# One row tile fewer in the experts, another order of VectorE's work and a hand-written last unit in the second layer

## The reference

```
# layer 0, on xn = layernorm(x)
q, k, v = split(xn @ W);  q = elu(q) + 1;  k = elu(k) + 1
s = (q @ (k^T v)) / (q . sum(k) + 1e-6)                       # linear attention, per batch row
e = argmax(xn @ gate_w^T)                                     # one of 8 experts per token
f = (square(relu(g)) * u) @ wd[e],  g = xn @ wg[e],  u = xn @ wu[e]
x = x + s * silu(f)

# layer 1, on xn = layernorm(x)
q, k, v = split(xn @ W_qkv)
p = exp(causal scores of blocks of 128 tokens - row maximum);  p = p / (sum(p) + 1e-6)
s = (p @ v) @ W_out^T + b_out
f = layernorm(xn + outs) * ln_g + ln_b     # outs: attention over the tokens that 16 heads chose
x = x + s * silu(f)
```

## Time and profile before

| | us |
|---|---|
| median of 3 runs | 522.12 (520.51 to 523.44) |
| the profiled execution | 517.94 |
| its span (first to last instruction) | 516.2 |
| TensorE busy | 499.0 (97%) |
| VectorE busy | 456.9 (89%) |
| ScalarE busy | 393.1 (76%) |
| GpSimd busy | 307.5 (60%) |
| granted TensorE clock, mean | 0.998 of full speed |

### The profile page before, as it was taken

The page is one execution under the profiler, slowest core; times in us unless marked ns, Lnnn a source line. Parts: engine busy times, 40 slices in busy tenths (PEclk is TensorE's granted clock), DMA queues, the critical chain, the costliest instruction groups (busy, mean ns, idle before and its releaser), DMA issues.

```text
span 516.2 us, 12184 instructions
## 1 busy us (share of the span) xinstructions
PE 499.0 (97%) x3576; PEld 461.1 (89%) x3576; DVE 456.9 (89%) x1420; ACT 393.1 (76%) x891; POOL 307.5 (60%) x367
## 2 busy tenths in 40 slices
PE   6899999999999999899999999999999999999995
PEld 5899999999999999799999988878888888888884
DVE  6899999999999987669988948989999999999985
ACT  4878878787878774567777856878888887888883
POOL 5568866777676877332222038887777787785200
PEclk9999999999999999999999999999999999999999
DMA  8942322222222115457778664266666555655311
GB/s 228 243 118 88 123 84 81 84 83 83 83 84 83 43 62 193 135 164 237 224 229 262 197 196 124 89 131 139 132 139 137 123 135 131 142 134 111 83 42 62
DMA packets 59415, 67.83 MB, mean 131 GB/s; under 512 B 11864, under 2 KB 53728, under 8 KB 59360
## 3 DMA queue, kind: packets, MB, share of 16 engines
q1 hardware_dynamic: 44416, 38.82, 24.7%
q0 software_dynamic: 14944, 28.32, 22.7%
HBM read 39.85 MB, written 27.26 MB: 130 GB/s over the span
## 4 chain that ended last, share of the span: by engine, by line
PE 78%; DVE 6%; SPq 6%; issue 3%; DMA 3%; ACT 1%; POOL 1%; POOLq 0%; DVEq 0%
PE v_ps L1464 9%; PE q_ps L1442 9%; PE s_ps L1484 5%; PE k_ps L168 3%; PE gu_ps L1123 3%; PE k_ps L169 3%; PE m_ps L168 3%; PE k_ps L170 3%; PE m_ps L170 3%; PE m_ps L169 3%; PE tq_ps L168 3%; PE tq_ps L169 3%; PE tq_ps L170 3%; PE tq_ps L400 3%; PE pa_ps L1495 3%
## 5 line engine op out<-in xcount | busy, mean ns | idle before, releaser
L1816 POOL DMA_INDIRECT four<-expert_rows,gather_u x64 | 69.5, 1086 | 38.1 <-DMA expert_rows<-y 19.5
L949 POOL DMA_INDIRECT sorted_rows<-xn,row_u x64 | 68.0, 1063 | 17.2 <-issue 13.9
L938 POOL TENSOR_TENSOR xn<-xn 128x512 fp32r<-128x512 f32 x32 | 43.2, 1350 | 30.7 <-ACT xn L563 30.4
L1464 PE MATMUL v_ps<-wvo,xt 128*128 128x256 f32 x256 | 60.6, 379 | 0.0
L1442 PE MATMUL q_ps<-xt,wqk 128*128 128x256 f32 x256 | 60.6, 379 | 0.0
L1579 ACT ACTIVATE xn2nd<-res,shift,rstd 128x256 f32<-128x256 f32 (+1 forms) x64 | 34.9, 593 | 26.7 <-DVE shift L1686 26.6
L1442 PEld LDWEIGHTS q_ps<-xt,wqk 128*128 128x128 f32 x256 | 48.5, 190 | 6.9 <-issue 0.4
L209 POOL DMA_DIRECT2D four<-sorted_rows x36 | 19.7, 548 | 56.6 <-issue 53.4
L1464 PEld LDWEIGHTS v_ps<-wvo,xt 128*128 128x128 f32 x256 | 46.3, 190 | 5.0
L1822 POOL DMA_DIRECT2D res<-in_L_attn_x x26 | 35.1, 1391 | 17.6 <-DVE res L1642 16.0
L1831 POOL TENSOR_TENSOR rstd<-var_eps,neg_half 128x4 f32<-128x4 f32 x32 | 36.6, 1143 | 11.9 <-DVE var_eps L1678 11.8
(11 more groups left out here) (260 smaller groups left out, 1748.1 us busy)
## 6 DMA issues: line engine op xcount, KB each, us to landing
expert_rows<-y SPq DMA_DIRECT2D x36, 256.0 KB, 3.1
four<-in_L_attn_x SPq DMA_DIRECT2D x32, 256.0 KB, 2.9
out_rows<-att SPq DMA_DIRECT2D x32, 256.0 KB, 2.1
res<-in_L_attn_x POOLq DMA_DIRECT2D x26, 256.0 KB, 4.9
four<-sorted_rows SPq DMA_DIRECT2D x36, 128.0 KB, 2.6
four<-sorted_rows POOLq DMA_DIRECT2D x36, 128.0 KB, 2.8
wdn<-in_L_ffn_wd SPq DMA_DIRECT2D x2, 512.0 KB, 7.4
sorted_rows<-res SPq DMA_DIRECT2D x8, 128.0 KB, 5.8
```

Of the source, the lines that this page charges most:

```text
L938: nc.gpsimd.tensor_tensor(xn2[:, s, 1], xn[:, i], xn2[:, s, 0].bitcast(F32), ALU.subtract).then_inc(g["xn_split"], 1)
L949: nc.gpsimd.indirect_dma_start(out=z.sorted_dram.ap(), out_offset=bass.IndirectOffsetOnAxis(ap=row_u[:, i // CU, k:k + 1], axis=0), in_=xn ...
L1464: m = nc.tensor.matmul(v_ps[:, t, :], xt[:, i % 2, k, t * P:(t + 1) * P], wvo[:, k, :], start=(t == 0 and k == 0), stop=(k == KD - 1), ski ...
L1816: nc.gpsimd.indirect_dma_start(out=moe[:, n % SLOTS, t, :], out_offset=None, in_=z.expert_dram.ap(), in_offset=bass.IndirectOffsetOnAxis(a ...
```

## The change

- `experts`: a helper `width(n)` gives 1 for the pair 35 and 2 for every other. All helpers and the store handle `width(n)` tiles, so the 72nd row tile is neither computed nor stored. The gather reads from the first 71 tiles of `expert_rows`.
- VectorE's step in `second_layer`: `base_divisor(n-1)` moves up between `norm_stats` and `stats_complete`; `invert_divisor(n-1)` moves from behind `maximum` to behind `find_moments`; `prepare_norm` moves behind `norm_shift`.
- First units: `norm_shift(2)` moves from step 0 to between `scale_rows(4)` and `sum_x(4)`. On GpSimd `add_x(6)` moves ahead of `gather(9)`.
- Last unit (31): the engines' steps run to unit 30, and the rest is written out tile by tile: `v` in two halves with `scores(31)` between them, each probability tile transposed, copied and multiplied by itself, with own PSUM banks for the two tiles, and two stores instead of one.

```diff
+    def width(n):
+        return 1 if isinstance(n, int) and n == PAIRS - 1 else 2
...
-                for u in range(2):
+                for u in range(width(n)):
...
                 if not normed:
                     norm_stats(*ahead)
+                base_divisor(*back)
+                if not normed:
                     stats_complete(*ahead)
                 gate(*back)
                 if not normed:
                     find_moments(*ahead)
-                base_divisor(*back)
+                invert_divisor(*back)
+                if not (isinstance(n, int) and n < 1):
+                    norm_shift(n + 2, at(i, 2))
                 if not normed:
                     prepare_norm(*ahead)
-                if not (isinstance(n, int) and n < 0):
-                    norm_shift(n + 2, at(i, 2))
                 scale_gate(*next_one)
                 maximum(n, i)
-                invert_divisor(*back)
                 gate_rows(*back)
...
-            first_rows(4, 4)
+            scale_rows(4, 4)
+            norm_shift(2, 2)
+            sum_x(4, 4)
...
+            add_x(6)
             gather(9)
-            add_x(6)
```

The last unit. TensorE, then ScalarE, VectorE and SyncE:

```diff
-            run(pe, 0, step, UNITS)
+            run(pe, 0, step, LAST - 1)
+            q(n, i)
+            last_value(0)
+            scores(n, i)
+            turn_probs(n - 1, at(i, -1))
+            last_value(1)
+            attend(n - 1, at(i, -1))
+            pe.wait_ge(g["pt_copied"], n)
+            for t in range(UT):
+                pe.wait_ge(g["p_ready"], UT * n + t + 1)
+                nc.tensor.transpose(last_pt[t], pr[:, i % 2, t, :], z.ident[:]).then_inc(g["pt_ready"], 1)
+            for t in range(UT):
+                pe.wait_ge(g["pt_copied"], n + t + 1)
+                pe.wait_ge(g["v_copied"], n + t + 1)
+                pe.wait_ge(g["a_begun"], n + t + 1)
+                nc.tensor.matmul(last_a[t], prt[:, i % 2, t, :], vo[:, i % 2, t, :], start=False, stop=True,
+                                 skip_group_check=True).then_inc(g["att_ready"], 1)
...
-            run(act, -1, step, UNITS)
+            run(act, -1, step, LAST - 1)
+            tanh(n, i)
+            begin_last(0)
+            copy_q(n, i)
+            exp(n - 1, at(i, -1))
+            last_copy(0, "v_ready", last_v, vo, "v_copied")
+            copy_probs(n - 1, at(i, -1))
+            begin_last(1)
+            exp(n, i)
+            last_copy(1, "v_ready", last_v, vo, "v_copied")
+            for t in range(UT):
+                last_copy(t, "pt_ready", last_pt, prt, "pt_copied")
...
-            run(dve, 3, step, UNITS + 1)
+            run(dve, 3, step, LAST - 1)
+            result(n - 2, at(i, -2))
+            gate(*back)
+            gate(n, i)
+            base_divisor(*back)
+            maximum(n, i)
+            invert_divisor(*back)
+            base_divisor(n, i)
+            gate_rows(*back)
+            invert_divisor(n, i)
+            result(*back)
+            for t in range(UT):
+                dve.wait_ge(g["att_ready"], n + t + 1)
+                nc.vector.scalar_tensor_tensor(att[:, i % SLOTS, t, :], last_a[t], inv[:, i % SLOTS, t:t + 1], zg[:, i % SLOTS, t, :], ALU.mult, ALU.mult).then_inc(g["gated"], 1)
+            for t in range(UT):
+                dve.wait_ge(g["gated"], n + t + 1)
+                nc.vector.tensor_tensor(att[:, i % SLOTS, t, :], att[:, i % SLOTS, t, :], z.res[:, UT * n + t, :], ALU.add).then_inc(g["out_ready"], 1)
...
+            for t in range(UT):
+                sp.wait_ge(g["out_ready"], LAST + 1 + t)
+                sp.dma_start(out_units[LAST][:, t], att[:, LAST % SLOTS, t]).then_inc(out_stored[LAST % SLOTS], 16)
```

More of the change, by code:

```diff
@@ L1017, in experts @@
     assert PAIRS == ROUNDS * QUAD and OWNERS + OCTET * len(OWNER_LOADS) == SLOTS
+    assert z.B * z.L % P == 0
+    def width(n):
+        return 1 if isinstance(n, int) and n == PAIRS - 1 else 2
     with ExitStack() as ctx:
@@ L1153, in experts_of @@
             def experts_of(n):
-                return [pe.snap(owners[(2 * n + u) % OWNERS], min_val=0, max_val=E - 1) for u in range(2)]
+                return [pe.snap(owners[(2 * n + u) % OWNERS], min_val=0, max_val=E - 1) for u in range(width(n))]
             def step(m):
@@ L1429, in sync @@
                 load(n, n)
-            run(sp, 0, step, UNITS + 1)
+            run(sp, 0, step, UNITS)
+            for t in range(UT):
+                sp.wait_ge(g["out_ready"], LAST + 1 + t)
+                sp.dma_start(out_units[LAST][:, t], att[:, LAST % SLOTS, t]).then_inc(out_stored[LAST % SLOTS], 16)
             for i in range(SLOTS):
-                sp.wait_ge(out_stored[i], 16 * UNITS // SLOTS)
+                sp.wait_ge(out_stored[i], 16 * (UNITS // SLOTS + (UT - 1 if i == LAST % SLOTS else 0)))
         def tensor(pe):
@@ L1544, in tensor, with last_value @@
             pe.wait_ge(g["folded_copied"], 2)
-            run(pe, 0, step, UNITS)
+            run(pe, 0, step, LAST - 1)
+            n, i = LAST, LAST % TURN
+            def last_value(t):
+                if t == 0:
+                    pe.wait_ge(g["v_copied"], n)
+                for k in range(KD):
+                    m = nc.tensor.matmul(last_v[t], xt[:, i % 2, k, t * P:(t + 1) * P], wvo[:, k, :], start=(k == 0), stop=(k == KD - 1))
+                m.then_inc(g["v_ready"], 1)
+            q(n, i)
[14 more added lines that the diff above has]
+                                 skip_group_check=True).then_inc(g["att_ready"], 1)
         def scalar(act):
@@ L1634, in scalar, with last_copy, begin_last @@
             act.wait_ge(z.set_up, 4)
-            run(act, -1, step, UNITS)
+            run(act, -1, step, LAST - 1)
+            n, i = LAST, LAST % TURN
+            def last_copy(t, ready, src, dst, done):
+                act.wait_ge(g[ready], n + t + 1)
+                nc.scalar.activation(dst[:, i % 2, t], src[t], ACT.Copy).then_inc(g[done], 1)
+            def begin_last(t):
+                if t == 0:
+                    act.wait_ge(g["gated"], n - 1)
+                else:
+                    act.wait_ge(g["q_copied"], n + 1)
+                nc.scalar.activation(last_a[t], z.eps_bias[:], ACT.Copy).then_inc(g["a_begun"], 1)
+            tanh(n, i)
[9 more added lines that the diff above has]
+                last_copy(t, "pt_ready", last_pt, prt, "pt_copied")
         def vector(dve):
```

47 lines of the change are left out of this document (32 added, 15 removed).

## The result

The changed kernel took 514.34 us, the median of 3 runs (513.58 to 514.72), against 522.12 us (520.51 to 523.44) before. The ratios here are as recorded and are not the quotients of the two medians; in this case the quotient is 0.985, inside the interval, and by the ratio the gain is 6.6 us and not 7.8.

What follows compares the result with a forecast made beforehand. TensorE, busy 97%, was taken as the bound, with VectorE holding the steady steps by a hair. Gains of 1.0 + 2.1 + 0.9 + 1.7 = 5.7 us took 522.12 to 516.4 us, range 513.8 to 520.2.

Steps and rivals of the forecast that it cites:

- Part 1: End of the experts: dropping the 72nd row tile brings the second layer's values 1.0 us earlier, bounds 0 and 1.3.
- Part 2 (a): First units: moving `norm_shift(2)` ahead of `sum_x(4)` and `centre_gate(1)` starts TensorE's turn earlier and saves 0.73 us.
- Part 2 (b): First units: issuing `add_x(6)` ahead of `gather(9)` removes VectorE's wait and TensorE's 1.53 us too-long step.
- the 0.15 for what is late next: First units: with the stall gone, `norm_shift(5)` and the normalising make TensorE's turn late, costing 0.1 to 0.2 us.
- nothing stalls: First units: `gather(9)` comes 1.4 us later, but its rows are used some 6 us after issue, so no wait follows.
- Part 3: Steady steps: VectorE's reordered list falls to about 5.68 us, TensorE becomes the bound, 0.9 us gained, bounds 0 and 1.2.
- rival A: Steady steps: VectorE's order gives nothing, steps stay at 5.93; total gain 4.2 us, 517.9 us; chance 0.15.
- Part 4: Last unit, 31: earlier scores, tile-by-tile work and a half-size last store save 1.7 us, bounds 0.8 and 2.1.
- B: Experts: the dropped tile is off the path, so its 1.0 us is not gained; 517.4 us; chance 0.12.
- C: First units and last unit: the change doesn't win there; total gain 1.9 us, 520.2 us; chance 0.12.
- D: Steady steps: `base_divisor` in its new place closes a loop through the exponentials; slower, 526.5 us; chance 0.04.
- such an offset is the same for both kernels: Total: the median's 4.2 us above the profiled execution was taken as unchanged, turning 512.2 us into 516.4 us.

Runs made afterwards that it cites:

- e3: The changed kernel with all 72 row tiles in the experts again; median 514.88 us, ratio to before 0.9928.
- e5: The changed kernel with GpSimd's `norm_scale(6)` moved ahead of `gather(10)`; median 514.68 us, ratio to before 0.9874.
- e6: The changed kernel with GpSimd's order `gather(10)`, `norm_scale(6)`, `add_x(8)`, so `add_x(8)` comes later; median 514.50 us, ratio to before 0.9874.
- e10: The same kernel as e6, run again on another chip beside the changed kernel; median 515.24 us, ratio to before 0.9899.
- e2: The changed kernel with VectorE's order in a step as before, all else as changed; median 513.37 us, ratio to before 0.9898.
- e7: The changed kernel with the last unit as before, loops running over unit 31 and one store; median 516.02 us, ratio to before 0.9896.
- e4: The changed kernel with `add_x(6)` behind `gather(9)` again; median 516.68 us, ratio to before 0.9967.
- e1: The changed kernel run again with no edit; median 514.55 us, ratio to the kernel before 0.9935.
- e11: The kernel before with one edit, `add_x(6)` ahead of `gather(9)`; median 518.68 us, ratio to before 0.9970.

## Why the prediction was right, point by point

**Part 1**, 1.0 forecast, 0.75 measured (e3 alone: 0.7 to 0.8). The half `gate_up` and the half `down` came as worked out, 0.45 and 0.24 to 0.25. What was mis-sized is the head start of 0.45 that `hidden(35)` was to have on VectorE. Ahead of it stand `silu(32)` and `silu(33)`, at 0.69 each and unchanged: `hidden(35)` starts on VectorE 1.23 us behind `gate_up(35)` (296.25), when the `silu` at 295.64 lets it, against 1.40 before (296.17), so 0.17 earlier where I had 0.45. The halved instructions gave 0.34 where I had 0.35: `hidden_rest(35)` starts 2.98 us behind `gate_up(35)` and not 3.36, of which 0.21 is theirs, and it is itself shorter, which gives 0.13. So `down(35)` comes 0.17 + 0.34 = 0.51 earlier and not 0.8.

**Part 2 (a)**, 0.73 forecast, 0.72 measured. `norm_shift(2)` at 322.67 ended the wait of the turn, with no other one behind it.

**Part 2 (b)**, 1.38 forecast after the 0.15 for what is late next, 1.34 measured at its own place. But the step "nothing stalls" behind `gather(9)` failed. I had asked when the gathered rows were wanted and not what else stands in GpSimd's list. Two gathers took 2.23 and 2.06 us instead of 1.0, `norm_scale(6)` slid to 346.86, and 1.1 us went at unit 6. The forecast's row showed the transfer; the row I lacked is GpSimd's own timeline of the next units, which up to the end of `norm_scale(6)` has no idle stretch over 0.31 us even before (334.30 to 345.73). Neither of the two other orders of GpSimd's list tried here, e5 and e6 with e10, avoids the debt for certain: one execution of e6 did better by 0.6, the next did not.

**Part 3**, 0.9 forecast, 1.07 measured, 5.873 us with VectorE's list at 5.65 and 0.22 of room. My working was loose: the three savings that it names, 0.12, 0.12 and 0.04, add up to 0.28 and not to the 0.23 that it goes on with, and the list fell by 0.26, from 5.91 to 5.65. For the size of the gain this hardly counts, since TensorE holds the step from 5.87 down. e2 decides between this part and rival A: the same instructions with the waits moved apart take 0.27 less a step. For the rival I had taken from the Trainium skill, "VectorE: DVE Perf Modes", section "The DRAIN you can't avoid", that waits cost nothing. That was half of what the section says: it also says that a next instruction that isn't held starts earlier, and with that half the trace agrees (0.05 us from the reciprocal to its follower, 0.19 where the follower waits). Rival A is refuted for the steps. In the total, though, e2 is only 0.5 to 0.7 behind, for part of it is what the stall at unit 6 takes. That the stall hangs on the order is shown, by seven traces with it and the one of e2 without; that it does so through the phase of the gathers against `scale_rows` is only argued.

**Part 4**, 1.7 forecast, 1.6 measured (e7: 1.6). The scores started at 503.34, 2.67 after `q(31)`, where I had 2.6. The end fell at 9.02 after `q(31)` against 8.85, and the store tail gave the 0.2 that I took for it; half the bytes by the fixed cost that the Trainium skill gives ("SBUF — State Buffer", section "The DMA setup-cost knee") would have given 0.3 by the prediction's estimate, close enough that this run can't tell the two apart.

**Rivals B and C** are out: the tile is on the path, and neither the first units nor the last gave back what they won except for the 1.1 us. **D** did not happen: VectorE waited at L1785 for an exponential only in the last units, 0.49 twice and 1.14 in unit 31. There `gate_rows(30)` behind it waited 0.32 more for its products, so the wait cost nothing.

**The total.** The parts sum to 0.75 + 0.72 + 1.34 + 1.07 + 1.56 = 5.44. Less 1.11 for the new stall it is 4.3, and 4.1 in the span with the 0.25 upstream. The forecast of the gain in the span was 1.6 too good, and that of the profiled execution, 512.2 against 514.72, 2.5: the other 0.9 is the time outside the span, which the prediction did not think of.

The median came out 2.1 better than forecast all the same, by the step that said such an offset is the same for both kernels. It was 522.12 - 517.94 = 4.2 before and 514.34 - 514.72 = -0.4 after, 4.6 us apart, more than the whole error of the parts. That the median lies in the range is therefore in good part luck. The range itself does not follow from its own terms: 2.7 and 6.5 us of gain with 1.5 on either side are 514.1 to 520.9, not 513.8 to 520.2, and the result is 0.2 us above the lower end of the first.

The changed kernel has medians of 514.34, 514.55 and 514.04 in the three sets that it ran in, and the kernel before 522.12, 518.47 and 520.03 in the same ones (520.91 in the fourth). The gain is 3.9 to 7.8 us by set, and it is before's time that moves. Why is not shown. With `add_x(6)` behind the gathers the stall was 1.5 us in one trace and 4.07 in another (e4), but these are two kernels, and e4's ten runs don't spread more (514.79 to 518.33) than e1's nine (513.22 to 517.48). e11, which takes only this place away, wins 1.35 us. A part goes with TensorE's clock: on the second and third chip, before's runs with a mean granted clock under 0.995 have median spans of 520.35 and 519.3 us (4 and 6 runs), those with 0.997 or more 518.5 and 518.2. No trace of such a run of before is on record, so where the clock fell in them, and the rest of before's excess over its profile, stay open.

## What to carry to other kernels

When an instruction is moved ahead in a full list, don't ask only when its own result is wanted: walk through every later instruction of that engine for two more steps and ask when each of theirs is wanted, with the durations that its kind has shown at worst. An order in which each follower waits for the instruction right ahead costs real time on an engine that is busy 98% of a step, and the gain ends where the next engine becomes the bound. A stall can also cost more than its own length: in e4, 2.31 us without work for TensorE was followed by 1.54 us lost to a lower clock. And a difference between two profiled executions is good to some tenths of a us where a stretch is compared, but not for the median: here the offset between the two was 4.2 us for one kernel and -0.4 for the other.

## What was not expected of the hardware

A gather's issue on GpSimd takes 0.94 us, and up to 2.23 us at certain phases of VectorE's work, the same ones in three executions; beside 14 VectorE instructions of one kind it never took more than 1.14. What lengthened it there was a one-input `tensor_scalar` (1.09 to 1.14) and not one with two SBUF inputs (0.94 to 0.96).

Small VectorE instructions of 0.13 to 0.16 us start 0.05 to 0.09 after each other when they are independent, and 0.19 when the follower waits for the one right ahead.

After an idle time of 2.31 us TensorE's granted clock was 0.59 of full speed over the next 3.93 us (e4); after one of 1.25 us in the kernel before it stayed at 1.00.
